# Two scans in a row every second step, with the decays prepared in even steps

## The reference, cut to what matters

```python
proj = hidden_states @ in_proj_w.T            # gate, x, B, C, dt
xBC = silu(causal_conv4(xBC) + conv_b)
dt = clip(softplus(dt + dt_bias), 0.001, 100.0)
cs = cumsum(dt * A)                           # in a chunk; A = -(1..128)
scores = (C @ B.T) * where(tri, exp(cs_i - cs_j), 0)
y = scores @ (x * dt) + (what the state brings) + x * D
yg = y * silu(gate)
out = (yg * rsqrt(mean(yg**2 over a group) + eps)) * norm_w @ out_proj_w.T
result = x + out * silu(experts(xn))          # xn = layernorm(x)
```

## Time and profile before

| | |
|---|---|
| median of 3 runs | 1608.88 us (1608.12 to 1609.1) |
| profiled execution | 1607.79 us |
| its span, first to last instruction | 1605.9 us |
| mean granted TensorE clock | 0.999 of full speed |
| PE busy | 1588.1 us, 99% |
| DVE busy | 1409.4 us, 88% |
| ACT busy | 1197.1 us, 75% |
| POOL busy | 960.3 us, 60% |
| chain that ended last | PE 85%, DVE 7%, ACT 3% |

### The profile page before, as it was taken

One profiled execution on the slowest core, in us unless ns is written; L12 is line 12 of the kernel. 1 busy time (PEld: TensorE's weight loads), 2 busy tenths in 40 slices (PEclk: granted clock), 3 DMA queues, 4 the chain that ended last, 5 costly groups with the idle time before them and its releaser, 6 DMA issues.

```text
span 1605.9 us, 28456 instructions
## 1 busy us (share of the span) xinstructions
PE 1588.1 (99%) x8478; PEld 1266.5 (79%) x8478; DVE 1409.4 (88%) x1654; ACT 1197.1 (75%) x2305; POOL 960.3 (60%) x596
## 2 busy tenths in 40 slices
PE   9999999999999999999999999999999999999998
PEld 6887777877778777877778777877778777877776
DVE  7726899889998899889998899889998899889987
ACT  4525978777887778777887778777887778778772
POOL 6522556656666656656666656656666656656563
PEclk9999999999999999999999999999999999999999
DMA  5234344334443344434443334334443344334432
GB/s 186 75 137 148 124 133 149 136 115 158 136 140 123 132 134 156 131 116 155 139 137 128 127 133 161 128 119 150 146 133 127 125 133 160 131 117 155 151 132 85
DMA packets 83831, 216.88 MB, mean 135 GB/s; under 512 B 10576, under 2 KB 12880, under 8 KB 83536
## 3 DMA queue, kind: packets, MB, share of 16 engines
q1 hardware_dynamic: 83376, 214.55, 39.6%
q10 hardware_dynamic: 288, 0.30, 0.1%
HBM read 209.83 MB, written 4.98 MB: 134 GB/s over the span
## 4 chain that ended last, share of the span: by engine, by line
PE 85%; DVE 7%; ACT 3%; issue 3%; POOL 1%; DMA 0%; ACTq 0%; SPq 0%; DVEq 0%; POOLq 0%
PE pj L454 15%; PE pj L456 15%; PE pj L455 15%; PE pr L454 9%; PE pr L455 8%; PE pr L456 8%; PE sc L699 7%; PE sc L703 3%; PE tb L688 3%; DVE conv L1368 2%; ACT decay L967 1%; DVE wo_lo L1432 1%; DVE decay L1396 1%; PE pr L677 1%; DVE xc L1382 1%
## 5 line engine op out<-in xcount | busy, mean ns | idle before, releaser
L1070 POOL TENSOR_TENSOR w_lo<-stg,w_hi 128x512 fp32r<-128x512 f32 x316 | 495.9, 1570 | 316.9 <-ACT w_hi L941 255.5
L454 PE MATMUL pj<-xT_hi,w_hi 128*128 128x512 f32 x1208 | 476.4, 394 | 6.3 <-DVE conv L1368 4.8
L456 PE MATMUL pj<-xT_hi,w_lo 128*128 128x512 f32 x1208 | 470.8, 390 | 0.0
L455 PE MATMUL pj<-xT_lo,w_hi 128*128 128x512 f32 x1208 | 470.4, 389 | 0.0
L1368 DVE SCALAR_TENSOR_TENSOR conv<-pj,par,conv 128x510 f32<-128x510 f32 (+2 forms) x480 | 357.7, 745 | 77.7 <-ACT conv L949 64.3
L967 ACT ACTIVATE decay<-decay,dtg 128x256 f32<-128x256 f32 (+1 forms) x1024 | 379.0, 442 | 0.0
L1107 POOL TENSOR_TENSOR xc<-xc,thg 128x512 f32<-128x512 f32 x128 | 203.2, 1587 | 188.7 <-DVE xc L1419 188.1
L1113 POOL TENSOR_TENSOR sqsum<-sqsum,sq 128x512 f32<-128x512 f32 x112 | 217.8, 1945 | 115.9 <-ACT sq L995 112.5
L454 PEld LDWEIGHTS pj<-xT_hi,w_hi 128*128 128x128 f32 x1208 | 226.7, 188 | 61.9 <-issue 6.5
L456 PEld LDWEIGHTS pj<-xT_hi,w_lo 128*128 128x128 f32 x1208 | 226.7, 188 | 48.1
L455 PEld LDWEIGHTS pj<-xT_lo,w_hi 128*128 128x128 f32 x1208 | 226.9, 188 | 45.4
(11 more groups left out here) (182 smaller groups left out, 1973.9 us busy)
## 6 DMA issues: line engine op xcount, KB each, us to landing
stg<-wstream SPq DMA_DIRECT2D x387, 256.0 KB, 2.7
decay<-cs_scr SPq DMA_DIRECT2D x128, 768.0 KB, 4.3
acc<-hid SPq DMA_DIRECT2D x8, 256.0 KB, 5.4
out<-acc SPq DMA_DIRECT2D x8, 256.0 KB, 2.0
dt_scr<-decay SPq DMA_DIRECT2D x1, 1024.0 KB, 6.6
gate_scr<-part SPq DMA_DIRECT2D x4, 256.0 KB, 2.0
dtg<-dt_scr SPq DMA_DIRECT2D x16, 64.0 KB, 4.0
stg<-hid SPq DMA_DIRECT2D x4, 256.0 KB, 4.7
```

The costliest lines, as they stand in the source:

```text
L454: nc.tensor.matmul(dst, hi_w, hi_x, start=first, stop=False)
L455: nc.tensor.matmul(dst, hi_w, lo_x, start=False, stop=False)
L456: return nc.tensor.matmul(dst, lo_w, hi_x, start=False, stop=last)
L1070: nc.gpsimd.tensor_tensor(w_dest(n, 1), stg[:, s % RING, :], f32(w_dest(n, 0)), ALU.subtract).then_inc(S["wl"], 1)
```

## The change

The scans of blocks s-1 and s are done together in odd steps s. To this end:

- TensorE: in even steps no scan. The scans write to the banks of the list `yb` (sc, tb, sc, pr[0], sc, pr[3], sc, pr[3] for blocks 0 to 7). There are new waits: a scan waits for `u` of one block less, an odd block's scan for the bank's last reader (`ms` for tb, `acc` for pr[0] and pr[3]), `out_first(0)` and `out_first(3)` and the turn of block 2 for the `add_scan` that reads their bank. In step 1 the turn of block 2 stands behind the out part.
- VectorE: both `block_weights` in even steps, that of block s behind `gate_silu`, and that of block s+1 behind `split_out_lo`; in odd steps `add_scan` of both blocks, and `x_times_dt(s+1)` behind them (in step 1 at the end); both `y_lo` of the pair in the even step that follows, the second at the end of the step; `add_output(3)` at the begin of step 5; in step 4 `add_output(2)` stays in front of the second `x_silu`.
- ScalarE: drops and decays for block s+1, not s+2; `y_hi` and `square` of both blocks of a pair in the even step that follows: y_hi, square, y_hi ahead of the late drops, the second square behind the decays.
- GpSimd: `gated` of both blocks in odd steps, both `add_square` in even steps.
- SyncE: exponents of blocks s+2 and s+3 in even steps.

```diff
+        yb = [sc, tb, sc, pr[0], sc, pr[3], sc, pr[3]]
...
-                if has_pair(g, half, s + 3):
-                    load_exponents(*pair(g, half, s + 3))
+                for n in (s + 2, s + 3):
+                    if s % 2 == 0 and has_pair(g, half, n):
+                        load_exponents(*pair(g, half, n))
... TensorE
+                if j == 2:
+                    pe.wait_ge(S["u"], at(g, half, NJ, 2))
...
-                pe.wait_ge(S["u"], at(g, half, NJ, j))
+                pe.wait_ge(S["u"], at(g, half, NJ, j - 1))
+                if j == 1:
+                    pe.wait_ge(S["ms"], at(g, half, 1, 0))
+                elif j % 2 == 1:
+                    pe.wait_ge(S["acc"], at(g, half, 4, 1 if j == 3 else 4))
...
+                if t in (0, 3):
+                    pe.wait_ge(S["u"], at(g, half, NJ, 4 if t == 0 else NJ))
...
-                if has_pair(g, half, s + 1):
+                if s != 1 and has_pair(g, half, s + 1):
                     x_turn(*pair(g, half, s + 1))
-                if has_pair(g, half, s):
+                if s % 2 == 1 and has_pair(g, half, s):
+                    scan(g, half, s - 1)
                     scan(g, half, s)
                 if len(mine) > 1:
                     channel_block(g, half, mine[1])
                 if with_out:
                     out_of_step(g, half, s)
+                if s == 1:
+                    x_turn(*pair(g, half, s + 1))
... ScalarE (drops and decays of s + 2 become s + 1)
+                if done:
+                    y_hi(*done[0])
+                    square(*done[0])
+                    y_hi(*done[1])
...
+                if done:
+                    square(*done[1])
... GpSimd
+                if s % 2 == 1 and has_pair(g, half, s):
+                    gated(g, half, s - 1)
                     gated(g, half, s)
... VectorE
+                if with_out and s == 5:
+                    add_output(*before, 3)
                 if has_pair(g, half, s):
                     gate_silu(g, half, s)
-                if has_pair(g, half, s + 1):
-                    block_weights(*pair(g, half, s + 1))
+                if s % 2 == 0 and has_pair(g, half, s):
+                    block_weights(g, half, s)
...
-                if has_pair(g, half, s + 1):
+                if s % 2 == 0 and has_pair(g, half, s + 1):
                     x_times_dt(*pair(g, half, s + 1))
-                if has_pair(g, half, s):
+                if s % 2 == 1 and has_pair(g, half, s):
+                    add_scan(g, half, s - 1)
                     add_scan(g, half, s)
+                if s % 2 == 1 and s != 1 and has_pair(g, half, s + 1):
+                    x_times_dt(*pair(g, half, s + 1))
                 for m in mine[1:]:
                     taps(g, half, m)
-                if s >= 1 and has_pair(g, half, s - 1):
-                    y_lo(g, half, s - 1)
+                if s >= 2 and s % 2 == 0 and has_pair(g, half, s - 1):
+                    y_lo(g, half, s - 2)
...
                     split_out_lo(g, half, s)
+                if s % 2 == 0 and has_pair(g, half, s + 1):
+                    block_weights(g, half, s + 1)
-                if with_out and 2 <= s <= 5:
+                if with_out and 2 <= s <= 4:
                     add_output(*before, s - 2)
                 for m in mine[1:]:
                     x_silu(*of_half(g, half, m), m)
+                if s == 1:
+                    x_times_dt(*pair(g, half, s + 1))
+                if s >= 2 and s % 2 == 0 and has_pair(g, half, s - 1):
+                    y_lo(g, half, s - 1)
```

More of the change, by code:

```diff
@@ L1004, in step @@
                         i = 1
-                    if has_pair(g, half, s + 2):
-                        drops(*pair(g, half, s + 2), 0)
+                    if has_pair(g, half, s + 1):
+                        drops(*pair(g, half, s + 1), 0)
                     gate_tanh(g, half, s)
-                elif has_pair(g, half, s + 2):
-                    drops(*pair(g, half, s + 2), 0)
-                if s >= 1 and has_pair(g, half, s - 1):
-                    y_hi(g, half, s - 1)
-                    square(g, half, s - 1)
-                if s == 0 and with_out:
[L1014 to L1018, removed]
+                elif has_pair(g, half, s + 1):
+                    drops(*pair(g, half, s + 1), 0)
+                before = (g, 0) if half == 1 else (g - 1, 1)
+                if s == 0 and with_out:
+                    done = [(*before, NJ - 2), (*before, NJ - 1)]
+                elif s >= 2 and s % 2 == 0 and has_pair(g, half, s - 1):
+                    done = [(g, half, s - 2), (g, half, s - 1)]
+                else:
+                    done = []
+                if done:
+                    y_hi(*done[0])
+                    square(*done[0])
+                    y_hi(*done[1])
+                if has_pair(g, half, s + 1):
+                    drops(*pair(g, half, s + 1), 1)
                 if mine:
@@ L1023, in step @@
                     i += 1
-                if has_pair(g, half, s + 2):
-                    decays(*pair(g, half, s + 2))
+                if has_pair(g, half, s + 1):
+                    decays(*pair(g, half, s + 1))
+                if done:
+                    square(*done[1])
                 if mine:
@@ L1052, in _ @@
                 step(G - 1, 1, s)
-            y_hi(G - 1, 1, NJ - 1)
-            square(G - 1, 1, NJ - 1)
+            for j in (NJ - 2, NJ - 1):
+                y_hi(G - 1, 1, j)
+                square(G - 1, 1, j)
         @block.gpsimd
@@ L1120, in step @@
                 if with_out and s == 0:
-                    add_square(*before, NJ - 1)
+                    add_square(*before, NJ - 2)
                 if with_out and s == 2:
                     inverse_rms(*before)
-                if s >= 2 and has_pair(g, half, s):
-                    add_square(g, half, s - 1)
+                if s >= 4 and s % 2 == 0 and has_pair(g, half, s):
+                    add_square(g, half, s - 2)
                 for i in range(1, n):
                     split_low(g, half, s, i)
-                if has_pair(g, half, s):
+                if with_out and s == 0:
+                    add_square(*before, NJ - 1)
+                if s >= 2 and s % 2 == 0 and has_pair(g, half, s):
+                    add_square(g, half, s - 1)
+                if s % 2 == 1 and has_pair(g, half, s):
+                    gated(g, half, s - 1)
                     gated(g, half, s)
@@ L1145, in _ @@
                 step(G - 1, 1, s)
+            add_square(G - 1, 1, NJ - 2)
             add_square(G - 1, 1, NJ - 1)
@@ L1465, in step @@
                     mask_products(*following(g, half))
-                if has_pair(g, half, s + 1):
+                if s % 2 == 0 and has_pair(g, half, s + 1):
                     x_times_dt(*pair(g, half, s + 1))
-                if has_pair(g, half, s):
+                if s % 2 == 1 and has_pair(g, half, s):
+                    add_scan(g, half, s - 1)
                     add_scan(g, half, s)
+                if s % 2 == 1 and s != 1 and has_pair(g, half, s + 1):
+                    x_times_dt(*pair(g, half, s + 1))
                 for m in mine[1:]:
                     taps(g, half, m)
-                if s >= 1 and has_pair(g, half, s - 1):
-                    y_lo(g, half, s - 1)
+                if s >= 2 and s % 2 == 0 and has_pair(g, half, s - 1):
+                    y_lo(g, half, s - 2)
                 if s == 0 and with_out:
-                    y_lo(*before, NJ - 1)
+                    y_lo(*before, NJ - 2)
                 if mine:
@@ L1485, in step @@
                     x_silu(*of_half(g, half, m), m)
+                if s == 1:
+                    x_times_dt(*pair(g, half, s + 1))
+                if s >= 2 and s % 2 == 0 and has_pair(g, half, s - 1):
+                    y_lo(g, half, s - 1)
+                if s == 0 and with_out:
+                    y_lo(*before, NJ - 1)
             def finish(n):
@@ L1527, in _ @@
             finish(3)
+            y_lo(G - 1, 1, NJ - 2)
+            finish(4)
             y_lo(G - 1, 1, NJ - 1)
-            finish(4)
             finish(5)
```

6 lines of the change are left out of this document (3 added, 3 removed).

## The result

The changed kernel takes 1659.53 us (median of 4 runs, 1657.81 to 1662.47) against 1608.99: a ratio of 1.0309, 95% interval 1.0295 to 1.0324. It is slower by about 50 us. The direction was forecast, the size was not: 1620 was predicted, with an upper end of 1636.

A forecast was written before the change was run, and what follows sets the result against it. PE, busy 99%, was taken as the bound, its stream nearly solid. 1607.8 - 22 (paired scans) + 31.5 (holes at bc_products) + 3 (other late DVE places) = 1620 us; range 1592 to 1636, the forecast's own 1611 to 1636.

The forecast's parts named there:

- 0.34 a pair: PE's scans done in pairs: 4.28 us for 4.62, so 0.34 us gained per pair, 22 us over 64 pairs.
- behind block_weights(5) and add_output(2): DVE in step 4: the second x_silu, which bc_products waits for, stands behind these two and comes late.
- stands for 2.1 us: PE at bc_products in step 5 of second halves: a hole of 2.1 us each.
- The term of 31.5 us for `bc_products`: PE's holes at bc_products summed over all halves: 31.5 us lost, with bounds of 13 and 50.
- Moved at no cost: SP's exponent fetches for two blocks in even steps, and other moved work, were claimed to cost nothing.
- 3 us in all: Other places where DVE is late: block 7's scan 1.6 us, half's start and kernel's end 1.4 us together.
- 0 to 4: Range for square_sums at a half's start and y_lo(6) at the kernel's end, together put at 1.4 us.
- 0 to 0.4 us, 8 times: PE's wait at the scan of block 7 in first halves for block_weights(7), 1.6 us in all.
- Rival 3: DVE bounds first halves' even steps, with holes at block 7's scan, half's start and bc_products: 1640 to 1652 us, chance 0.06.

The follow-up runs named there:

- bwlast: The changed kernel with VectorE's block_weights of the next step moved behind add_output and the second x_silu in even steps; 1631.18 us, ratio 1.0114.
- spread: The changed kernel with SyncE fetching the exponents of one block in each step, not of two in even steps; 1655.07 us, ratio 1.0279.
- best: bwlast plus exponents fetched one step at a time, both last y_lo ahead of every finish, and two VectorE instructions of step 4 moved; 1610.06 us, ratio 0.9999.
- extra4: The kernel before the change plus one more 768 KB transfer to scratch behind the exponents in step 4 of each first half; 1624.05 us, ratio 1.008.

## Why the prediction was wrong

**Right.** "0.34 a pair" of PE (0.34 measured; 21 us for 22 in all, as step 1 gave 0.28). The place and the cause of the main hole, "behind block_weights(5) and add_output(2)", shown by bwlast. Its size in second halves, "stands for 2.1 us": 2.33.

**The term of 31.5 us for `bc_products`** stands against 24.0 us of holes above before. The second halves came out as forecast (16.3 for 14.7), and so did groups 0 and 7 (6.0 more than before, for 6.3). The six first halves between them were given 10.5 and had 1.7, because PE was already late there by the pause at the branch; spread, without that pause, has 15.2 in them.

Inside that term two more errors met. `block_weights` was taken at 1.67 to 2.2, and it lasted 2.85; in return `x_silu` took 0.68 for 1.12, and the taps of x1 began 5.28 behind the turn, where 5.49 was forecast. The 2.85 has its cause beside it. POOL, in after:

```profile
686.32 1.84 POOL L1095 TENSOR_TENSOR w_lo<-stg,w_hi 128x512 fp32r<-128x512 f32 x1 [0.46 <-ACT w_hi L959]
```

It ends at 688.16, and from there to the end of `block_weights` (689.78) it is 1.62, not much less than an undisturbed one (1.75). It looks as if DVE could begin only when POOL let go. The other rows of this multiplication in after bear it out. Of its 128, 29 took 2.25 to 2.85 us; each of them began in the middle of a `w_lo` or `add_square` of POOL and ended 1.61 or 1.62 us behind that one's end. 36 had a POOL instruction begin inside them and took 1.75 all the same. The Trainium skill (GPSIMD Engine Reference, Specifications) has GpSimd and VectorE share SBUF interfaces, with contention for DVE instructions with two inputs in SBUF. These rows agree; I had weighed the rule before and placed the value below it.

**Wrong, first: "Moved at no cost. SP fetches exponents for two blocks in even steps."** For the data this is true. The step asked only what the transfer waits for and who uses it, and not what else shares the DMA engines while 1.5 MB go through. What does is the code of PE's loop. By the pauses it is 18.8 us of holes for 2.5 before; by the runs it is 12.4 us of the time (7.7 to 17), once the other hole no longer covers it.

**Wrong, second: a hole was priced at its length.** The sum had no term for what PE does after a hole. The 11 half-clock stretches behind holes make 17.5 us. bwlast shows the cost in one and the same kernel: its executions at a mean clock of 0.9905 took 9.4 us longer than those at 0.9955, and the clock alone gives 0.005 x 1630, about 8.

**Mis-sized: the places called "3 us in all".** The end was given "0 to 4" with `square_sums`; it measured 7.4 in the output's products, half clock included (6.2 us in time), and 3.1 at `square_sums`. I had seen that `y_lo` of block 6 stands behind `finish(2)` and `finish(3)`, but not that `finish(0)` and `finish(1)` are ahead of step 7, whose pair of scans now carries two blocks. "0 to 0.4 us, 8 times" in front of block 7's scan was right: no wait on decays stands in after's list.

In time, by the medians, from after to best: 28.4 us for the place of `block_weights` (with the half clock behind its holes), 12.4 for the exponents, 6.2 for the end, 2.5 for step 4, together 49.5. How the first two share their 40.8 is uncertain by some 5 us, as bwlast stands between them. The kernel before is then reached, and not passed. Rival 3 (1640 to 1652) has the nearest number, with another mechanism: the further holes are at the loop's branch and not at block 7's scan.

## What to carry to other kernels

When an instruction is moved, look at everything queued between the consumer's wait and what it waits for, all its semaphores included: moving one of two awaited instructions gained nothing, moving the one in front of both gained some 28 us. Price a transfer's new time also by who else uses the DMA engines then, the fetch of code at a loop's branch among them, and a hole in PE by its length plus a share of a stretch at half clock. Effects seen in one trace do not add: the same edit was worth 4.5 us with another hole behind it and 12.4 us without.

## What the runs showed of the hardware

- The branch of PE's loop took 7.56 us on its sequencer (584.80 to 592.36) while two fetches of 768 KB and a load of weights were under way, and 4.08 us passed between two products of PE (4.02 us and 0.55 in the same turn of before). In the kernel before one such transfer, added next to the branch, made 1.8 to 2.9 us of pause in each of six turns (+13 us); one that ended 14 us ahead of it, none.
- A pause of some 2.3 us in PE's stream could be followed by 3.4 us at 1.2 GHz, 1.6 us lost each. Of seven pauses of equal length, three had it. The same kernel (bwlast) ran at a mean clock of 0.990 to 0.996 and in 1636 to 1626 us.
- A DVE multiplication of 128 x 1536 with two operands in SBUF took up to 2.85 us and not 1.75 where it began in the middle of a `w_lo` or `add_square` of POOL, and ended 1.61 or 1.62 us behind that one's end, 29 times of 29. Where the POOL instruction began later than it, it took 1.75.
- The profile can name a wrong releaser: the pause at the branch is put down to DVE's `conv` in after and to "issue" in extra4.
